# First layer's setup: only the first batch's modulated rows before the layer's block, the rest inside it, and ten unread products on TensorE

## The reference

```python
mod = silu(c) @ wmod            # 16 x 1536: shift, scale, gate, twice
h   = layernorm(x) * (1 + scale1) + shift1
x   = x + gate1 * branch1(h)    # the same again for branch 2
```

## Time and profile before

| | us |
|---|---|
| median of 3 runs | 3178.84 |
| lowest and highest | 3176.0 and 3182.64 |
| the profiled execution: its time | 3183.52 |
| its span in the trace | 3181.8 |
| setup block, up to POOL's first work in the next block | 29.12 |
| from there to the first row maxima (L1081) | 16.20 |

### The profile page before, as it was taken

How to read it: one execution, slowest core, us unless ns; L and a number is a source line. 1 busy time by engine, 2 the same in 40 slices (tenths; PEclk the granted TensorE clock), 3 DMA queues, 4 the chain that set the end, 5 groups by cost and what they waited for, 6 DMA issues and landing times. The chain is left out here.

```text
span 3181.8 us, 58120 instructions
## 1 busy us (share of the span) xinstructions
PE 3018.6 (95%) x19338; PEld 1850.6 (58%) x19338; DVE 2186.8 (69%) x6717; ACT 1562.6 (49%) x3529; POOL 1213.6 (38%) x1530
## 2 busy tenths in 40 slices
PE   7899999999998998899999999999999968999997
PEld 3566766666665674344444444444444327888886
DVE  6777777777763333678888888888888842445545
ACT  3566556565552113466666666666666631111111
POOL 3123232232234212234444444444443242455544
PEclk8899999999999999899999999999999989999998
DMA  8111010110122981222222222222222217999995
GB/s 292 7 53 45 33 64 33 33 64 33 35 100 79 315 297 52 71 58 68 73 74 74 75 71 73 73 77 78 78 78 73 80 35 213 242 272 280 272 263 173
DMA packets 291041, 354.70 MB, mean 111 GB/s; under 512 B 49855, under 2 KB 240562, under 8 KB 290752
## 3 DMA queue, kind: packets, MB, share of 16 engines
q1 hardware_dynamic: 261760, 313.28, 31.2%
q0 software_dynamic: 28464, 34.71, 5.0%
q10 hardware_dynamic: 544, 3.15, 0.3%
HBM read 234.02 MB, written 122.34 MB: 112 GB/s over the span
## 5 line engine op out<-in xcount | busy, mean ns | idle before, releaser
L2907 DVE TENSOR_REDUCE negmax<-psum 128x1 f32<-128x512 f32 x1024 | 670.7, 685 | 129.7 <-PE psum L3487 125.1
L2520 ACT ACTIVATE pT<-psum 128x512 f32<-128x512 f32 x1024 | 576.8, 600 | 258.8 <-PE psum L3513 225.4
L3487 PE MATMUL psum<-k_stack,q_stack 96*128 96x512 bf16 x1024 | 357.0, 388 | 17.4 <-DVE negmax L2907 10.3
L3513 PE MATMUL psum<-q_stack,k_stack 99*128 99x512 bf16 x1024 | 347.8, 382 | 8.1 <-ACT pT L2520 6.2
L4149 POOL DMA_INDIRECT src_rows<-ye,place x142 | 221.9, 1563 | 283.3 <-DVE ye L4208 251.7
L990 ACT ACTIVATE probs<-probs,negmax 128x256 f32<-128x256 f32 x512 | 252.8, 495 | 119.0 <-DVE negmax L1081 117.4
L4166 ACT ACTIVATE actT_x<-psum 128x512 f32<-128x512 f32 x142 | 84.8, 597 | 441.4 <-PE psum L4323 441.4
L3527 PE MATMUL psum<-pT,v_tile 128*32 128x512 f32 x2048 | 273.3, 606 | 1.6 <-ACT pT L2520 1.0
L4323 PE MATMUL psum<-xT_x,w_x 128*128 128x256 f32 x1136 | 260.3, 383 | 1.1 <-DMA w_x<-in_L_ffn_w_dram 1.1
L4335 PE MATMUL psum<-w_x,actT_x 128*128 128x256 f32 x1136 | 256.6, 379 | 0.0
L1081 DVE CUSTOM_DVE_ANT_0 probs<-psum,band_mask 128x256 f32<-128x256 f32 x512 | 181.6, 421 | 104.8 <-PE psum L1339 104.7
(11 more groups left out here) (420 smaller groups left out, 5602.8 us busy)
## 6 DMA issues: line engine op xcount, KB each, us to landing
w_x<-in_L_ffn_w_dram SPq DMA_DIRECT2D x142, 512.0 KB, 5.4
w_e<-in_L_ffn_w_dram SPq DMA_DIRECT2D x46, 1024.0 KB, 6.4
q_stacks<-q_part SPq DMA_DIRECT2D x192, 128.0 KB
q_stack<-q_stacks SPq DMA_DIRECT2D x64, 384.0 KB, 3.7
padded<-w_e SPq DMA_DIRECT2D x32, 650.0 KB, 6.0
xe<-padded SPq DMA_DIRECT2D x71, 260.0 KB, 5.2
gate_rows<-mods SPq DMA_DIRECT2D x66, 256.0 KB, 5.6
src_e<-src_rows SPq DMA_DIRECT2D x30, 512.0 KB, 6.5
```

The lines of the kernel that those rows point to most:

```text
L2520: act.activation(pT[:, 4 * (s % 2) + r, :], bank(m, 2 + n % 2), ACT.Exp, scale=float(DHQ) ** -0.5)\
L2907: dve.tensor_reduce(negmax[:, p // REP, h:h + 1], bank(m, max_bank(b, 16 * g + p)), AX.X, ALU.max, negate=True).then_inc(max_read, 1)
L3487: pe.matmul(bank(m, max_bank(b, 16 * g + p)), q_stack[0:K_SCORE, h, t * P:(t + 1) * P], k_stack[0:K_SCORE, g, :], start=True, stop=True).t ...
L3513: pe.matmul(bank(m, 2 + n % 2), k_stack[:, g, kc * P:(kc + 1) * P], q_stack[:, REP * g + r, :], start=True, stop=True).then_inc(sT_done, 1)
```

## The change

`setup_tiles` lays the tiles that must outlive setup (layer 1's `wmod1`, `condT`, `mod0`, `rows0`, the biases, the routing inputs and constants) into the part of `m.x` that belongs to batches 7 to 15; SP's load of batch 7 (`LATE`) waits until these are read. Setup keeps the conditions, layer 0's six products, the norm of batch 0, and two of four groups of columns. Ten products of the identity with itself, which nothing reads, come first on PE, and the identity is made first on POOL. Layer 1's products and the counting of experts go to PE's stream in the layer's block, the routing casts to DVE's, the copies to ACT's; the making of the nine rows goes from DVE to POOL (`first_rows`), and their store to SP's stream there. Layer 1's `wmod` goes from ACT's queue to SP's, and the small loads and the routing loads to the end of SP's setup stream.

```diff
-    m.mod_cols0 = sb("mod_cols0", [P, 4, C, B])
+    m.mod_cols0 = sb("mod_cols0", [P, 2, C, B])
...
+    late = m.x[:, LATE * (NT * D):]
+    taken = [0]
...
+    m.wmod1 = room(C * 6 * D).rearrange("p (c n) -> p c n", c=C)
+    m.condT = room(2 * C * B).rearrange("p (l c b) -> p l c b", l=2, c=C)
+    m.mod0 = room(6 * D)[0:B, :].rearrange("b (s d) -> b s d", d=D)
...
-            load_batch(0)
...
+            load_x(sp, m, I, 0, m.x_first)
+            load_attention_weights(sp, m, I)
+            sp.dma_start(m.wmod1[:, :, :], I["L1_wmod"].rearrange("(c p) n -> p c n", p=P)).then_inc(m.x_second, 16)
+            load_x(sp, m, I, 1, m.x_second)
-            load_batch(1)
+                sp.dma_start(m.bias0[:, i, :], I[n].partition_broadcast(B)).then_inc(m.bias1_in, 16)
...
-            sp.wait_ge(rows_ready, 8)
-            sp.dma_start(mods_dram[0, :, :, :], rows[:, :, :]).then_inc(m.rows_out, 16)
+            load_small_weights(sp, m, I)
...
             pool.memset(m.ident[:, :], 0.0).then_inc(zeroed, 1)
             pool.memset(m.ident_bf[:, :], 0.0).then_inc(zeroed, 1)
-            pool.memset(m.band_mask[:, :, :], 0.0).then_inc(zeroed, 1)
-            pool.memset(m.ones_col[:, :], 1.0).then_inc(constants, 1)
-            pool.wait_ge(zeroed, 3)
+            pool.wait_ge(zeroed, 2)
             for eye in (m.ident, m.ident_bf):
                 pool.affine_select(out=eye[:, :], in_=eye[:, :], compare_op=ALU.not_equal, fill=1.0, base=0,
                                    pattern=[[-1, P]], channel_multiplier=1).then_inc(constants, 1)
+            pool.memset(m.band_mask[:, :, :], 0.0).then_inc(zeroed, 1)
+            pool.memset(m.ones_col[:, :], 1.0).then_inc(constants, 1)
...
+            act.dma_start(wmod[:, :, :], I["L0_wmod"].rearrange("(c p) n -> p c n", p=P)).then_inc(wmod_in, 16)
...
-            act.wait_ge(rank_done, 1)
...
-                act.wait_ge(mod_done, NBLK + n + 1)
-                act.activation(m.mod1[:, 2 * n:2 * n + 2, :].rearrange("b s d -> b (s d)"), bank(m, NBLK + n)[0:B, :],
-                               ACT.Copy)
...
-            modulation_gates(step, dve, mod[:, :, :], sign[:, :, :], rows[:, :, :], scaled=True)
...
+            dve.wait_ge(mod_read, 1)
+            dve.tensor_scalar(m.mod0[:, 1, :], m.mod0[:, 1, :], 1.0, None, ALU.add).then_inc(scale_ready, 1)
...
-            pe.wait_ge(constants, 5)
+            pe.wait_ge(constants, 2)
+            for _ in range(10):
+                pe.matmul(bank(m, 0)[:, 0:P], m.ident[:, :], m.ident[:, :], start=True, stop=True)
...
+            pe.wait_ge(wmod_in, 16)
...
             pe.wait_ge(m.xn0_ready, NT)
-            pe.wait_ge(mod_read, 2)
             for c in range(C):
                 for t in range(NT):
                     mm = pe.transpose(bank(m, c)[:, t * P:(t + 1) * P], m.xn[:, t, c * P:(c + 1) * P], m.ident[:, :])
                 mm.then_inc(m.hT_done, 1)
+            pe.wait_ge(scale_ready, 1)
+            for i in (0, 1):
+                for c in range(C):
+                    j = (i * C + c) * B
+                    mm = pe.transpose(bank(m, 6)[:, j:j + B], m.mod0[:, i, c * P:(c + 1) * P], m.ident[0:B, 0:B])
+            mm.then_inc(cols_done, 1)
...
+            load_mlp_weights(sp, m, I)
+            sp.wait_ge(rows0_ready, 8)
+            sp.dma_start(mods_dram[0, :, :, :], m.rows0[:, :, :]).then_inc(m.rows_out, 16)
             sp.wait_ge(m.rows_out, 16)
             load_norm_rows(0)
             load_gate_rows(0)
-            load_mlp_weights(sp, m, I)
+            sp.wait_ge(m.x_third, 32)
             for b in (2, 3):
                 load_x(sp, m, I, b, m.x_third)
             load_norm_rows(1)
             for b in range(4, B):
+                if b == LATE:
+                    sp.wait_ge(mod1_done, 3)
+                    sp.wait_ge(rank_done, 1)
                 load_x(sp, m, I, b, m.x_rest)
             sp.wait_ge(zeros_ready, 2)
             clear(0)
...
+            def first_rows():
+                mod, sign, rows, bias = m.mod0, m.sign0, m.rows0, m.bias0
+                gates = mod[:, 2:6:3, :]
+                step = Steps(pool, rows0_s, 0, 0)
+                step(pool.tensor_scalar(sign[:, :, :], gates, 0.0, 0.5, ALU.is_ge, ALU.subtract))
+                pool.wait_ge(m.bias1_in, 16 * 7)
+                step(pool.tensor_tensor(bias[:, 0, :], bias[:, 0, :], bias[:, 2, :], ALU.add))
+                step.settle()
+                step(pool.tensor_tensor(gates, gates, sign[:, :, :], ALU.mult))
+                pool.tensor_scalar(rows[:, 7, :], mod[:, 4, :], 1.0, None, ALU.add).then_inc(rows0_ready, 1)
+                step.settle()
+                step(pool.tensor_scalar(gates, gates, 0.125, 4.0, ALU.max, ALU.mult))
+                pool.tensor_copy(rows[:, 8, :], mod[:, 3, :]).then_inc(rows0_ready, 1)
+                step.settle()
+                step(pool.tensor_tensor(rows[:, 0:3:2, :], gates, sign[:, :, :], ALU.mult))
+                pool.tensor_copy(rows[:, 4, :], mod[:, 1, :]).then_inc(rows0_ready, 1)
+                step.settle()
+                step(pool.tensor_tensor(rows[:, 3, :], rows[:, 2, :], bias[:, 1, :], ALU.mult))
+                step(pool.tensor_tensor(rows[:, 1, :], rows[:, 0, :], bias[:, 0, :], ALU.mult))
+                step.settle()
+                step(pool.tensor_tensor(sign[:, 0, :], rows[:, 3, :], m.later0.to_broadcast([B, D]), ALU.mult))
+                pool.tensor_tensor(rows[:, 6, :], rows[:, 0, :], bias[:, 4, :], ALU.mult).then_inc(rows0_ready, 1)
+                pool.tensor_tensor(rows[:, 5, :], mod[:, 0, :], bias[:, 3, :], ALU.add).then_inc(rows0_ready, 1)
+                step.settle()
+                pool.tensor_tensor(rows[:, 1, :], rows[:, 1, :], sign[:, 0, :], ALU.add).then_inc(rows0_ready, 3)
+
+            first_rows()
             hidden_rows(0, 0)
...
+            for n in range(3):
+                act.wait_ge(mod1_done, n + 1)
+                act.activation(m.mod1[:, 2 * n:2 * n + 2, :].rearrange("b s d -> b (s d)"), bank(m, 2 + n)[0:B, :], ACT.Copy)\
+                    .then_inc(mod1_read, 1)
+            act.wait_ge(rank_done, 1)
+            ranks = bank(m, 0)[:, 0:2 * NSORT * E].rearrange("p (a j e) -> p a j e", a=2, e=E)
+            act.activation(m.rank0, ranks[:, 0, :, :], ACT.Copy).then_inc(ranks_read, 1)
+            act.activation(m.total0, ranks[:, 1, :, :], ACT.Copy).then_inc(ranks_read, 1)
+            act.activation(m.scan0[:, 0, :, :], ranks[:, 1, :, :], ACT.Copy).then_inc(ranks_read, 1)
             body(0, 0, prev=False)
...
+            dve.wait_ge(m.x_third, 32)
+            place(dve.tensor_copy(m.token0[:, :], m.token_i0[:, :]))
+            place(dve.tensor_copy(m.route_f[:, :], m.route_i[:, :]))
+            place(dve.tensor_copy(m.iota_f0, m.iota_i0[:, :]))
+            place.settle()
...
+            dve.wait_ge(m.x_second, 32)
             first_norm0(dve, m, 1, first_keys_values)
+            dve.wait_ge(ranks_read, 3)
             body(0, 0, first=True)
...
+            pe.wait_ge(m.x_second, 32)
+            second_modulation(0)
             pe.wait_ge(hT_act, 1)
             pe.wait_ge(hT_dve, 1)
             project_inputs(m.wq0, 0, 0, 7, q_done)
             project_inputs(m.wq0, 1, 0, 5, q_done)
             project_inputs(m.wk0, 0, 0, 6, k_done)
+            second_modulation(1)
             pe.wait_ge(q_ready, 1)
             project_inputs(m.wk0, 1, 0, 7, k_done)
+            second_modulation(2)
             pe.wait_ge(q_ready, 2)
             project_values(0, 0, 5)
+            count_experts()
             pe.wait_ge(k_ready, 1)
             project_values(1, 0, 6)
+            pe.wait_ge(mod1_read, 3)
+            pe.wait_ge(ranks_read, 3)
             body(0, 0, first=True)
             body(1, 1, second=True)```

`count_experts` is the two products of L502 and L503 in bank 0, and `second_modulation(n)` is the two products of one group of 512 columns in bank 2 + n.

PE, from its first instruction to the first scores of the layer's block, ahead of the change (`x2T<-...` at L502: the hits; L516: `xn` of batch 0):

```order
L489 MATMUL psum<-ident,cond 128x16 [waits cond_in,constants]
L489 MATMUL psum<-ident,cond 128x16 x3
L496 MATMUL psum<-wmod,condT 16x512 [waits wmod_in0,condT_ready]
L496 MATMUL psum<-wmod,condT 16x512 x5
L502 MATMUL psum<-x2T,before 128x128 [waits hit_ready]
L503 MATMUL psum<-x2T,ones 128x128
L496 MATMUL psum<-wmod,condT 16x512 [waits wmod_in1]
L496 MATMUL psum<-wmod,condT 16x512 x5
L509 MATMUL psum<-ident,mod 128x16 [waits scale_ready]
L509 MATMUL psum<-ident,mod 128x16 x7
L516 MATMUL psum<-ident,xn 128x128 [waits mod_read,first_norm_ready]
L516 MATMUL psum<-ident,xn 128x128 x7
```

More of the change, by code:

```diff
@@ L314, in setup_block @@
         cond = sb("cond", [B, 2, D])
[L315 to L333 removed]
+        wmod = sb("wmod", [P, C, 6 * D])
+        expT = sb("expT", [P, 2 * C * B])
         cond_in = sem("cond_in")
[L335 to L336 removed]
+        wmod_in = sem("wmod_in0")
         zeroed = sem("zeroed")
```

(48 more changed lines are left out.)

143 lines of the change are left out of this document (58 added, 85 removed).

## The result

| | median of 20 | lowest to highest | profiled span |
|---|---|---|---|
| before | 3182.28 us | 3176.0 to 3190.09 | 3181.8 |
| after | 3186.51 us | 3180.07 to 3193.33 | 3186.1 |

The ratio is 1.0016, 95% interval 1.0009 to 1.0024: slower, by 5 us (the medians lie 4.2 apart), under the 0.2% bound but clear of its own interval. Forecast was a gain of 0.7 us, and a median of 3178.1 within 3172.0 to 3185.5; it came 1.0 us above the top of that. The kernel before has moved up by 3.4 us against the three runs that the forecast was made from; that part of the miss is a matter of the sample, the wrong direction is not.

The account below looks back on a forecast made before the run. The head was taken to decide, up to VectorE's first row maxima, with POOL's chain ending last. Terms +0.4 and -1.1 gave -0.7 us, 3182.8 profiled, median 3178.1, range 3172.0 to 3185.5.

Parts of the forecast that it names:

- nothing behind the second batch is touched: Whole kernel: any gain or loss must be there by the first row maxima and is carried through unchanged blocks.
- Part 3: POOL's and SP's chain behind T: 25.9 us to the first row maxima, at 45.7 against 45.32, +0.4 us.
- Part 1: Setup block: 9.3 us shorter, ending at 19.8 us, bounds 17 and 24.
- if the upper clock is on: Setup, layer 0's products on PE: 12 records last 5.4 us at the upper clock, otherwise 10.8.
- T: The moment setup ends and POOL starts on `kT`: 29.12 us before, 19.8 forecast.
- Part 2: PE, ACT and DVE behind T: PE busy to T + 18, so maxima could start at T + 20 = 39.8.
- the new `xn`, 1.3: End of the head's chain: 1.3 us from the end of POOL's multiplication to the first row maxima.
- Part 4: Counting of experts: POOL's later work slides, some five VectorE steps run with it idle; gain 1.1 us (0 to 2).
- (a): Rival, head: the reserve is not used up, POOL's 16-row operations cost as VectorE's; about -8.6 us, 3170; chance 0.14.
- (b): Rival, setup: PE stays at the lower clock; maxima at 50.1, 3182.5 us; chance 0.13.
- (c): Rival, end of setup: small loads at the end of SP's stream hold the barrier; T = 25.7, 3185.5 us; chance 0.11.

Follow-up runs that it names:

- e1_pad15: The changed kernel with 15 one-cell fills added at the start of VectorE's setup code; ratio to the kernel before 0.9999.
- e13_zeros_moved: The changed kernel with SyncE's stores of zeros issued behind the load of the next norm rows; ratio to the kernel before 0.9993.
- e14_both_zeros_moved: The changed kernel with rows 4 and 5 made first, GpSimd's first-batch addition waiting for VectorE's normalised rows, and the zero stores moved; ratio to the kernel before 0.9979.

## Why the prediction was wrong

**Where it failed:** its premise, "nothing behind the second batch is touched", and blocks "that run as they did". The work behind was the same, its code lay elsewhere, and VectorE stood 3.96 us for a fetch that SyncE's burst held up, in place of 1.12. That was worth 2.9 us behind the loop and 5.0 to 6.5 us by the end of the block by the profiles, and 5 us by the times with and without fills, which is about the whole loss. The second step that failed is a term of Part 3, below.

**Part 1** held. PE began at 2.00, and the products, 4.63 us instead of 6 (0.23 a record), cost the path nothing instead of 1.2. Layer 0's took 5.32 us for 5.4 forecast, but this was luck: the repeat of the same kernel took 8.18, so the term "if the upper clock is on" is not settled by the unread products. The prediction's reading that the first set of the kernel before began at the lower clock is not borne out either. Single records of 0.59 to 1.06 us would fit two levels, but the granted clock is shown as 1.00 in every stretch up to 20 us, in the repeat too. As it is 1.00 even ahead of TensorE's first instruction, that row may not tell much here, and why the records are slow is open. x was there at 9.0 (8.5). T was 20.46 (19.8; bounds 17 and 24), for the reason named, SP's list, with two stalls of 2.22 and 4.18 us. **Part 2** held: scores from 39.20, ready at 40.35, for 39.8.

**Part 3** named the chain and sized GpSimd's rows right: 12.97 us for 13.1, store and load 6.13 for 6.4 (2.8 + 3.6). The mis-sized term is the last, "the new `xn`, 1.3". It was read where GpSimd and VectorE did not meet. In the new chain GpSimd's addition and VectorE's `xn` start on the same event, so they always meet: 3.0 or 4.1 us from `xn`'s start to the maxima, which makes 47.5 to 48.0 or 48.3 to 49.0 instead of 45.7. The earlier trace rows already showed a copy at 0.70 beside GpSimd, and Part 4 used it for a gain only.

**Part 4**'s saving of 1.1 us (0 to 2) was about 2.3 in the first kind of run (the counting steps fell from 4.74 to 2.35 us), which is how a head 2.4 us late left +0.1 at 134 us, and between -0.8 and +0.7 in the second.

**The rivals.** (a) and (b) did not come. (c) named SP's list, but T stayed far from 25, and no loss shows from 134 us on. (Its price is 0.3 us too high: 3178.8 + 7.5 - 1.1 is 3185.2.) The slower side came by a way on no list.

**Still open:** why before's own stall of 1.12 us comes at all and e1_pad15, with VectorE's code in the same place, has none; why a stall costs 1.12, 1.56 or 2.5 us with no data moving; and how the second part of the loss arises. Between 890 and 1022 us the five profiles with the long stall lose another 1.8 to 3.6 us, those with no stall 1.1 to 1.6, and all others -1.5 to +0.2, e13_zeros_moved (-0.5) and e14_both_zeros_moved (-0.2) with the same code place among them. So it goes with the long stall, but no one wait or clock carries it: in after TensorE's granted clock is 0.68 from 970 to 980 (1.00 before), in the repeat it is 1.00 there.

## What to carry to other kernels

An edit at the head moves the code of everything behind it: where an engine leaves a loop, and for a while behind it, look at "issue" idle time and at the packets of the instruction queues, and keep bursts of transfers away from there. A wait of TensorE costs more than its length where the clock falls with it. When work goes from VectorE to GpSimd, price what VectorE then does beside it, above all where one event starts both; to let GpSimd wait 1.4 us cost nothing that could be measured, and the first maxima came 2 us earlier. And of rows made for a store, make those first whose reload is waited for.

## What was new about the hardware

- A fetch of code, 8 KB, kept VectorE idle for 3.93 to 4.12 us where SyncE's burst ran (1.0 MB moved ahead of the packet in after), for 2.51 and 2.56 us with the zeros moved out of its way (0.3 MB in e13), and with no data moving for 2.52, 1.56 or 1.12 us, or not at all.
- TensorE's wait of 2.28 us was followed by a granted clock of 0.69 and 0.50 and cost another 1.8 us; a wait of 0.88 us in the same place left the clock at 1.00.
- VectorE's four 128x256 rows take 1.37 us alone and either 2.7 to 3.1 or 4.21 us beside GpSimd's additions; in both kinds they start 0.02 to 0.03 us ahead of them.
- Ten float32 products of 128 columns ahead of twelve of 512 did not fix their time: 5.3 to 8.3 us with them, 6.96 to 7.88 without.
